# Convolution with f32 messages and marks in one product, 128-row gathers, two additions in one

## The reference

```python
h = relu(layernorm(x))
R = relu(edge_weight[:, None] @ w1 + b1) @ w2 + b2        # 200000 x 384: weights by edge
Y = spherical_harmonics(edge_attr_3)                      # from the edge's vector
Fj = h[src]                                               # 200000 x 32
msg = for each edge: products of R (8x8 by path), Y and Fj: 8 scalars and 8 vectors of 3
out[dst] += msg                                           # sum by destination
x = x + out
```

## Time and profile before

| | us |
|---|---|
| median of 3 runs (11203.65 to 11251.74) | 11221.48 |
| the profiled execution: time | 11271.17 |
| its span | 11269.5 |
| VectorE busy | 9343.8 (83%) |
| TensorE busy | 7516.8 (67%) |
| GpSimd busy | 5206.8 (46%) |
| ScalarE busy | 3160.2 (28%) |

### The profile page before, as it was taken

The page is one execution under the profiler, slowest core; times in us unless marked ns, Lnnn a source line. Parts: engine busy times, 40 slices in busy tenths (PEclk is TensorE's granted clock), DMA queues, the critical chain, the costliest instruction groups (busy, mean ns, idle before and its releaser), DMA issues.

```text
span 11269.5 us, 344658 instructions
## 1 busy us (share of the span) xinstructions
PE 7516.8 (67%) x130038; PEld 5063.0 (45%) x130039; DVE 9343.8 (83%) x19419; ACT 3160.2 (28%) x7975; POOL 5206.8 (46%) x5783
## 2 busy tenths in 40 slices
PE   2555555400877877877877887786777777777773
PEld 2444444300766766766766776674222222222221
DVE  8777777668877877877877877777999999999995
ACT  0111111048222222222222222222444444444441
POOL 3777777610321321221221231133877777777771
PEclk9999999975988988988988988896555555555555
DMA  4111111157644744754754655562222222222221
GB/s 173 25 25 25 26 25 25 30 176 242 206 150 149 212 148 149 210 152 149 212 149 151 198 171 161 167 200 60 37 36 36 36 35 36 36 36 34 36 34 19
DMA packets 719352, 1177.38 MB, mean 104 GB/s; under 512 B 177346, under 2 KB 340241, under 8 KB 715001
## 3 DMA queue, kind: packets, MB, share of 16 engines
q1 hardware_dynamic: 435480, 1024.95, 28.7%
q0 software_dynamic: 146832, 68.64, 5.8%
q10 hardware_dynamic: 136012, 67.95, 2.4%
HBM read 1018.50 MB, written 140.22 MB: 103 GB/s over the span
## 4 chain that ended last, share of the span: by engine, by line
PE 31%; DVE 24%; issue 19%; ACT 3%; POOL 2%; DVEq 1%; DMA 1%; ACTq 0%; POOLq 0%; SPq 0%
PE psum L1964 10%; PE psum L1932 10%; PE psum L1947 6%; DVE space L1444 3%; DVE space L1478 2%; PE psum L2039 2%; DVE space L1440 2%; DVE space L1477 2%; DVE space L1412 2%; PE psum L2009 2%; ACT space L1595 2%; DVE space L1482 2%; DVE space L1489 2%; DVE space L1422 2%; PE psum L2024 1%
## 5 line engine op out<-in xcount | busy, mean ns | idle before, releaser
L792 POOL DMA_INDIRECT space<-feature_table,space x2000 | 2422.6, 1211 | 615.2 <-issue 614.9
L717 POOL TENSOR_TENSOR claim_out<-claim_in 128x1 f32<-128x1 f32 x1199 | 309.7, 258 | 4533.3 <-DMA table<-space 2424.7
L2055 PE MATMUL psum<-w_mix,space 64*128 64x448 f32 x4144 | 1833.8, 982 | 0.0
L1627 ACT ACTIVATE space<-psum 128x375 f32<-128x375 f32 x2400 | 938.8, 435 | 2885.3 <-PE psum L1932 2880.6
L728 POOL DMA_INDIRECT slots<-space x1568 | 1511.6, 964 | 465.4 <-issue 412.1
L1143 DVE TENSOR_TENSOR space<-psum,space 128x320 f32<-128x320 f32 x2400 | 1066.4, 486 | 748.6 <-PE psum L1947 722.7
L1932 PE MATMUL psum<-space 128*32 128x125 fp8e4 x72000 | 1342.5, 223 | 239.5 <-issue 238.2
L1964 PE MATMUL psum<-space 128*128 128x96 bf16 x24000 | 1289.7, 207 | 220.6 <-issue 159.9
L1932 PEld LDWEIGHTS psum<-space 128*32 128x32 bf16 x72000 | 1077.2, 97 | 494.1 <-issue 484.7
L1964 PEld LDWEIGHTS psum<-space 128*128 128x128 fp8e4 x24000 | 1101.1, 97 | 379.4 <-issue 263.3
L1153 DVE TENSOR_TENSOR space<-space 128x320 f32<-128x320 f32 x2400 | 1062.7, 484 | 1.4 <-DVE space L1149 1.1
(11 more groups left out here) (278 smaller groups left out, 11875.5 us busy)
## 6 DMA issues: line engine op xcount, KB each, us to landing
space<-marks SPq DMA_DIRECT2D x2400, 320.0 KB
marks<-space SPq DMA_DIRECT2D x100, 640.0 KB, 3.2
space<-distances ACTq DMA_DIRECT2D x200, 320.0 KB
space<-block_ids SPq DMA_DIRECT2D x198, 200.0 KB
slots<-space SPq DMA_DIRECT2D x82, 448.0 KB, 9.7
space<-feature_table,space POOLq DMA_INDIRECT x2072, 2.7
space<-src_rows SPq DMA_DIRECT2D x102, 320.0 KB, 4.0
slots<-space POOLq DMA_INDIRECT x1608, 2.1
```

The source lines that it names most:

```text
L792: g.indirect_dma_start(out=gathered_rows[0:SLOTS, half, t, :], out_offset=None, in_=feature_table, in_offset=bass.IndirectOffsetOnAxis(ap= ...
L1627: a.activation(to[:, s0:s1, :, :], pair_picked[:, bank, 0:(s1 - s0) * PICK_COLS].rearrange("p (k c r) -> p k c r", k=s1 - s0, r=CAP), ACT.Copy
L2055: last = mm(radial[:, 2 * ring + odd, 0:MIX_S + MIX_V], hidden[odd * HIDDEN:(odd + 1) * HIDDEN, slot, upper * LANES:(upper + 1) * LANES], ...
```

## The change

- The marks are f32 and the message is one f32 word: one f32 product per tile in place of three bf16 ones. The two subtractions that made the parts go; the last reduction signals `messages_ready`. The products' buffers move.
- `spread` and `framed` share memory. What kept them apart was a wait ahead of the subtractions; now the projection waits for `messages_ready` of the group before, which starts at 1.
- The two additions that make two thirds of `coefs` become one over both, with a broadcast operand; for that, the order and a sign of two columns of the mixed weights are changed, and the projection's sum and difference with them.
- The gathers and the copy of their indices go over 128 lanes, not 125.

```diff
-        edge_words = conv_space(3 * GROUP * PARTS * D)
+        edge_messages = conv_space(3 * GROUP, D)
...
-                    g.indirect_dma_start(out=gathered_rows[0:SLOTS, half, t, :], out_offset=None, in_=feature_table,
+                    g.indirect_dma_start(out=gathered_rows[:, half, t, :], out_offset=None, in_=feature_table,
                                          in_offset=bass.IndirectOffsetOnAxis(
-                                             ap=row_index[0:SLOTS, half, t:t + 1], axis=0)
+                                             ap=row_index[:, half, t:t + 1], axis=0)
...
-            def project_plus(kind, g, summed):
+            def project_apart(kind, g, summed):
...
-                return kind.chain.mark(v.tensor_tensor(z[:, :, 4, :], z[:, :, 2, :], z[:, :, 3, :], ALU.add))
+                return kind.chain.mark(v.tensor_tensor(z[:, :, 4, :], z[:, :, 3, :], z[:, :, 2, :], ALU.subtract))
...
                 if ahead:
+                    dve.wait_ge(messages_ready, nth + 1)
                     framed_ready = project(kind, i + (g + 1) // kind.groups, nxt)
...
-                v.tensor_tensor(coefs[:, :, :, 1], sum_v[:, :, :, 0], sum_v[:, :, :, 2], ALU.subtract)
-                chain(v.tensor_tensor(coefs[:, :, :, 2], sum_v[:, :, :, 0], sum_v[:, :, :, 1], ALU.add))
+                chain(v.tensor_tensor(coefs[:, :, :, 1:3], sum_v[:, :, :, 0:1].to_broadcast([LANES, GROUP, U, 2]),
+                                      sum_v[:, :, :, 1:3], ALU.add))
...
-                vectors = chain.mark(v.tensor_reduce(
+                v.tensor_reduce(
                     row[:, :, U:D].rearrange("p t (u o) -> p t u o", o=3),
-                    spread[:, :, :, :].rearrange("p t (u f) o -> p t u o f", f=3), AX, ALU.add))
+                    spread[:, :, :, :].rearrange("p t (u f) o -> p t u o f", f=3), AX, ALU.add).then_inc(messages_ready, 1)
...
-                chain.after(vectors)
-                chain(v.tensor_tensor(left, row, tops[0], ALU.subtract))
-                v.tensor_tensor(least, left, tops[1], ALU.subtract).then_inc(messages_ready, 1)
...
-                pe.wait_ge(messages_ready, nth + 1)
+                pe.wait_ge(messages_ready, nth + 2)
...
-                    for c in range(PARTS):
-                        last = mm(conv_sums[:, tile // SUM_BLOCKS, to:to + D], lane_marks[:, ring, :],
-                                  edge_halves[:, BUFFER_OF[g] * GROUP + t, c, :, 1], start=False, stop=True,
-                                  skip_group_check=True)
+                    last = mm(conv_sums[:, tile // SUM_BLOCKS, to:to + D], lane_marks[:, ring, :],
+                              edge_messages[:, BUFFER_OF[g] * GROUP + t, :], start=False, stop=True,
+                              skip_group_check=True)
```

More of the change, by code:

```diff
@@ L399, in build_gnn @@
         spill_dist = hgT[0:SPILL_PART, 0, 0:LANES]
-        assert 2 * UNIT_TILES * REC <= 1024 and SPILL_PART * LANES <= 2 * FAR_WORDS and bias_at + 4 * (MIX_S + MIX_V) <= 3840
+        assert 2 * UNIT_TILES * REC <= 1024 and SPILL_PART * LANES <= 2 * FAR_WORDS and bias_at + 4 * (MIX_S + MIX_V) <= 5120
         psum = ctx.enter_context(nc.psum_tensor("psum", [LANES, 8 * BANK], F32))
@@ L854, in _ @@
             v.engine_nop().then_inc(quad_added, 2)
+            v.engine_nop().then_inc(messages_ready, 1)
             v.engine_nop().then_inc(spill_sums_added, 2)
@@ L1360, in _ @@
                     (scal[:, U:2 * U, U:2 * U], path11[:, :, :, 2], norm1 * 3.0 * quad),
[L1361 to L1362 removed]
+                    (vect[:, :, 2, :], path11[:, :, :, 0], norm1 * y0 * delta),
+                    (vect[:, :, 1, :], path11[:, :, :, 1], -norm1 * c1 * cross)):
                 step(v.tensor_scalar(dst_ap, src_ap, factor, None, ALU.mult))
[L1364 removed]
+            step(v.scalar_tensor_tensor(vect[:, :, 2, :], path11[:, :, :, 2], -norm1 * quad, vect[:, :, 2, :],
                                         ALU.mult, ALU.add))
[L1366 to L1367 removed]
+            step(v.tensor_tensor(scal[:, U:2 * U, U:2 * U], scal[:, U:2 * U, U:2 * U], vect[:, :, 2, :], ALU.add))
+            v.tensor_tensor(vect[:, :, 0, :], vect[:, :, 2, :], vect[:, :, 1, :], ALU.subtract).then_inc(wide_ready, 1)
             bias = w2_mix[HIDDEN:HIDDEN + 1, :]
@@ L1453, in group_step @@
                 parts_at = slice(BUFFER_OF[g] * GROUP, (BUFFER_OF[g] + 1) * GROUP)
-                row, left, least = (edge_parts[:, parts_at, c, :] for c in range(PARTS))
-                tops = [edge_halves[:, parts_at, c, :, 1] for c in range(PARTS)]
+                row = edge_messages[:, parts_at, :]
                 dve.wait_ge(scalars_copied, nth + 1)
@@ L1466, in group_step @@
                 if ahead:
-                    plus = project_plus(kind, nxt, summed)
+                    apart = project_apart(kind, nxt, summed)
                 if ahead and kind is Main and nxt in (2, 4):
@@ L1473, in group_step @@
                 if ahead:
-                    minus = project_minus(kind, nxt, plus)
+                    joint = project_joint(kind, nxt, apart)
                 if kind is Main:
@@ L1500, in first_project @@
                 summed = project_sums(kind, 0, framed_ready)
-                plus = project_plus(kind, 0, summed)
-                kind.chain.after(project_minus(kind, 0, plus))
+                apart = project_apart(kind, 0, summed)
+                kind.chain.after(project_joint(kind, 0, apart))
             def move_sums(j):
@@ L1748, in copy_index @@
                     act.wait_ge(scalars_copied, PAIR_GROUPS * i - 2 + 2 * half)
-                a.activation(row_index[0:SLOTS, half, :],
-                             slot_row[0:SLOTS, bass.ds((2 * i + half) * UNIT_TILES, UNIT_TILES)],
+                a.activation(row_index[:, half, :],
+                             slot_row[:, bass.ds((2 * i + half) * UNIT_TILES, UNIT_TILES)],
                              ACT.Copy).then_inc(index_copied, 1)
@@ L2120, in add_over @@
                         own = slice(half * HALF, (half + 1) * HALF)
-                        for c in range(PARTS):
-                            last = mm(half_sums[:, 2 * (g % 2) + half, t * D:(t + 1) * D], lane_marks[own, ring, :],
-                                      edge_halves[own, BUFFER_OF[g] * GROUP + t, c, :, 1], start=c == 0,
-                                      stop=c == PARTS - 1)
+                        last = mm(half_sums[:, 2 * (g % 2) + half, t * D:(t + 1) * D], lane_marks[own, ring, :],
+                                  edge_messages[own, BUFFER_OF[g] * GROUP + t, :], start=True, stop=True)
                 last.then_inc(quad_added, 1)
```

29 lines of the change are left out of this document (13 added, 16 removed).

## The result

The changed kernel takes 11189.4 us (median of 7 runs, 11173.08 to 11193.58) against 11228.19 us (7 runs, 11203.65 to 11251.74) of the kernel before: ratio 0.9955, interval [0.9944, 0.9966]. It is faster, by 0.45% where 1.2% were forecast. The profiled execution has a span of 11187.8 us.

The account below looks back on a forecast made before the run. VectorE was taken to set the pace, with TensorE's longer add taking back half its saving. Main convolution -140, chunk ends +8, overflow +6, first gathers -4: -130 us from the 11221.5 us median, giving 11091 us, range 10960 to 11200.

Parts of the forecast that it names:

- VectorE's saving: Main convolution: two subtractions gone and two additions made one save 1.01 us a group, 12.72 to 11.71 us without waits.
- The addition: VectorE, each group: one addition of 128 elements with a broadcast replaces two of 64, saving 0.08 us.
- the f32 instruction at 0.157 us: TensorE's add: load and columns add up, 0.157 us an instruction at 32 columns, so 16 take 2.51 us.
- the upper bound of the prediction: TensorE's add: cost doesn't fall below that of 64 columns, 0.2135 us an instruction, 3.42 us for 16.
- rival B: Add at 0.2135 us an instruction: fourth multiply at 6.07 us, group 13.12 us, total 11331 us; chance 0.11.
- the clock of the add and its pair: TensorE in the main convolution: add and the radial pair behind it both priced at half clock, pair 2.35 us.
- A: Add hidden by overlapped weight loads or full clock; VectorE alone sets the pace, turn 59.1 us, total 10967 us; chance 0.21.
- rival C: Both effects cancel: an add near 3 us, -10 to -50 us, total 11190 us; chance 0.10.
- The wait, in sum: VectorE's fourth multiply starts at 5.16, not 4.66 us; half of 1.01 us saved comes back as waiting, group 12.21 us.
- Chunk ends: At 5 chunk ends VectorE's wait for the add grows by 1.9 us; together +8 us.
- Overflow stage: Behind the convolution: 9 groups save 1.0 us each on VectorE, adds grow from 0.8 to 2.5 us; +6 us.
- Gathers: With 128 rows 0.96 in place of 1.21 us; GpSimd just doesn't bind; first 16 gathers bring -4 us.

Follow-up runs that it names:

- experiment 1: The kernel before with 128-row gathers and the one addition, marks and messages still bf16 in three parts: 11201.71 us, ratio 0.9976 to before.
- Experiment 7: The kernel before with 128-row gathers, the one addition and messages as two bf16 parts in place of three: 11091.21 us, ratio 0.9864 to before.
- experiment 3: The changed kernel with the add's f32 products over 16 of the message's 32 columns: 11186.76 us, ratio 0.9962 to the kernel before.
- experiment 4: The changed kernel with the first 64 of the 128 columns of marks as the add's weights: 10939.29 us, ratio 0.975 to the kernel before.

## Why the forecast was right in direction and wrong in size

- **VectorE's saving: right.** Forecast 11.71 us for a group without a wait, measured 11.68. The addition was forecast at 0.08 us and brings 0.10 (12.71 to 12.61 in experiment 1), over 250 groups some 25 us. That is nearly the whole gain of the convolution, 26 to 31 us. Experiment 7 confirms the price of a subtraction.
- **The failed step: the f32 instruction at 0.157 us, and so the add at 2.51 us.** At half clock the add takes 3.35 us. I drew a line through a 64-column and a 448-column distance as if an f32 instruction cost a load and its columns. The runs show 0.21 us at 32 columns and at 16 alike (experiment 3), and 0.11 with 64 weight columns (experiment 4). It is the upper bound of the prediction, 0.2135 from rows 4, that was right: the product there has 64 moving columns and 128 weight columns, and its distance was that of the weights already. The line through it followed the wrong variable. The argument against rival B, that transposes of 128 columns and products of 64 have the same distance, is just what a distance set by the weights gives. The one short distance of 0.11 us in rows 4 stays unexplained. With 0.2135 the sum of the prediction gives rival B's 6.07 us for the fourth multiply; measured 5.89, which is 0.14 to the start of the add (not 0.20), 3.35 to the next product, 2.35 for the pair and 0.05.
- **Second failed step: the clock of the add and its pair, priced at half always.** In the kernel after, 116 of 217 adds start at full clock, and in these groups VectorE waits less or not at all. That is most of why the whole did not come out at B's 11331 us; the rest is the overflow stage, priced there at +13 us. B's group of 13.12 us holds for the half of the groups whose add starts at half clock. A's state is rare: only 12 of 204 groups have add and pair both at full clock (median 11.8 us). The sentence that gave A its chance, that TensorE would stand idle hardly 0.3 us a group, does not follow from rows 3: 2.67 - 1.01 - 0.9 (an add of 1.7 in place of 0.80) is about 0.8 us. The measured 11189.4 us is what rival C said (11190 us, an add near 3 us, both effects cancel), and the mean add, from its start to the next product, does take 3.1 us. But C was given 0.10 and no mechanism, and this mean is a mixture of adds of some 2.3 us (started at full clock) and 3.5 us (at half); that C has the very number is partly luck.
- **The wait, in sum.** Forecast 0.50 us a group, so that half of the saving was kept. Measured 0.86 us idle, and each waiting multiply also loses the 0.08 us by which it would overlap its predecessor (9508.37 + 0.74 against 9509.03): 0.86 + 146 x 0.08 / 203 = 0.92 us. The 0.42 us beyond the forecast are 105 us over 250 groups, most of what is missing of the 130 us. The product saves 0.93 us on VectorE. What is left, some 0.01 us a group, is less than what the chunk ends cost.
- **Chunk ends:** forecast +1.9 us each, measured +2.7 (1.12 to 3.85), 14 us in all: the add's length again.
- **Overflow stage:** forecast +6 us, measured -6 (257.0 to 250.8 us from the last move of sums to the end of the span). An add there grew from 0.83 us to 3.6, more than forecast, but VectorE's waits for the pair grew only from 21.9 to 27.7 us and those at the adds fell from 11.1 to 9.2: +4 us, not +15, against 9 us saved. As many multiplies wait as before, 15. I had charged the add's whole growth to each of 9 groups from one wait of 0.59 us; why most of it is hidden there was not tested.
- **Gathers:** the size was right (0.97 us), the first two waits for rows fell by 2.2 (13.25 to 11.04) and 2.0 us (7.16 to 5.16), 4 in all as forecast, and GpSimd still waits for VectorE. Not binding, as forecast.

The Trainium skill, TensorE: Matmul & The Clock Gate, LDWEIGHTS, gives a load as columns / 1.2 ns and names no type there: 107 ns for 128 columns. The f32 distances here at half clock go with the weight columns, as it says, and are twice as long, 0.21 and 0.11 us; the measurement decides. The same page, Weight-path perf modes, says that the fast load of weights is for 128 columns and types other than FP32. The 24 bf16 products of before in 0.80 us, 0.033 us each with the same 128 columns, agree with that; the prediction had not weighed this rule, which speaks against the change.

## What to carry to other kernels

Turning three bf16 products into one f32 product of few moving columns saves no TensorE time when each product has its own weights: count two f32 weight loads for each product, by the columns of the weights. When an engine off the path gets longer work, look at what is queued right behind that work and who waits for it: here 0.93 us saved on VectorE came back as a wait for a pair that had 1.1 us to spare. The remedy is order (half of the add behind the pair) or the clock, and each must be tried alone before both.

## What the hardware showed that was not expected

- An f32 instruction with 128 weight columns costs 0.21 us at half clock (1.2 GHz) whether 16, 32 or 64 columns move; at full clock 0.11 us (1.83 us for 16).
- From 8200 to 10800 us the changed kernel has TensorE busy 2330 us and a mean granted clock of 0.60; with zeros ahead of the adds it is busy 2403 us and the clock 0.78. Work that computes nothing pays for itself: 2.15 to 2.95 us of zeros a group, and the kernel is 1.3% faster than without them (11034.62 against 11184.64, measured side by side).
- A gather of 128 rows is shorter than one of 125 (0.97 and 1.21 us, same table).
- The same program can be 8% slower on another chip, and a change that gains 1.6% on one loses 11% on the other.
